# A decoder megakernel on one core: where the last encoder layer applies its third norm, and how top-k attention removes the scores that were not chosen

## The reference, cut to what matters

```python
xb = _layernorm(xb + o, g1[l], be1[l])            # first norm
ff = relu(xb @ W1[l].T + b1[l]) @ W2[l].T + b2[l]
xb = _layernorm(xb + ff, g2[l], be2[l])           # second norm
...
x = _layernorm(x + _L1_attn_ref(x, ...))          # third norm, once, behind the last layer
```

```python
scores = einsum('bthd,bghd->bhtg', Q, K) / sqrt(32)
scores = where(vision_mask, scores, -inf)
topv, topi = top_k(scores, 32)
probs = softmax(topv)
attn = zeros_like(scores).at[bi, hi, ti, topi].set(probs)
c_t = einsum('btg,bgd->btd', attn.mean(axis=1), x_vision @ Wv)
```

## Time and profile before

| what | value |
|---|---|
| time, median of 3 (lowest, highest) | 2394.77 us (2393.81, 2398.04) |
| the profiled execution | 2396.02 us, its span 2394.2 us |
| busy: PE, DVE, ACT, POOL | 88%, 63%, 30%, 34% of the span |
| encoder's last layer and its end | about 1508 to 1727 us |
| top-k attention, first `max` to the last `attend` | 1733.40 to 2050.49 us |

### The profile page before, as it was taken

How to read it: one execution, slowest core, us unless ns; L and a number is a source line. 1 busy time by engine, 2 the same in 40 slices (tenths; PEclk the granted TensorE clock), 3 DMA queues, 4 the chain that set the end, 5 groups by cost and what they waited for, 6 DMA issues and landing times.

```text
span 2394.2 us, 37754 instructions
## 1 busy us (share of the span) xinstructions
PE 2103.9 (88%) x15300; PEld 1469.6 (61%) x15300; DVE 1514.4 (63%) x3047; ACT 711.3 (30%) x1407; POOL 810.4 (34%) x726
## 2 busy tenths in 40 slices
PE   6988979999999978999999999988567767879986
PEld 2334337777766656888888888776445555446632
DVE  7998955566333325556556555666398998737556
ACT  6445324333311222232223222222142222121132
POOL 3242448966500014444444444432270000013101
PEclk9768689999899989999999999999766675889998
DMA  5222173222010027101001000100231110310001
GB/s 154 70 75 90 57 161 92 60 67 71 7 53 1 1 94 173 34 1 69 1 2 51 19 1 1 52 1 1 71 100 29 30 30 25 87 49 1 0 0 31
DMA packets 67181, 114.47 MB, mean 48 GB/s; under 512 B 34153, under 2 KB 58722, under 8 KB 65794
## 3 DMA queue, kind: packets, MB, share of 16 engines
q1 hardware_dynamic: 67010, 112.07, 16.3%
HBM read 91.56 MB, written 33.34 MB: 52 GB/s over the span
## 4 chain that ended last, share of the span: by engine, by line
PE 64%; DVE 25%; POOL 6%; issue 3%; ACT 2%; DMA 0%; SPq 0%; DVEq 0%; POOLq 0%; ACTq 0%
PE PS L1534 8%; PE PS L1550 8%; PE PS L1280 5%; PE PS L1258 4%; DVE top L2334 4%; DVE w_s L2343 4%; PE PS L2214 2%; DVE ln_st L270 2%; PE PS L2204 2%; PE PS L1447 2%; PE PS L1461 2%; PE PS L2143 2%; PE PS L892 2%; PE PS L879 2%; PE PS L409 2%
## 5 line engine op out<-in xcount | busy, mean ns | idle before, releaser
L289 POOL TENSOR_SCALAR ln_ve<-ln_mv 128x2 f32<-128x2 f32 (+1 forms) x87 | 20.0, 230 | 1195.5 <-DVE ln_mv L273 1195.4
L1807 POOL TENSOR_TENSOR q_x<-q_f,cols 128x2048 f32<-128x2048 f32 x56 | 217.9, 3911 | 9.7 <-ACT q_f L1638 8.0
L1762 DVE TENSOR_TENSOR p_x<-PS,cols 128x1024 f32<-128x1024 f32 x112 | 129.3, 1218 | 134.3 <-PE PS L1496 134.3
L1089 DVE TENSOR_REDUCE XD<-PS 112x2 f32<-112x750 f32 x128 | 120.0, 940 | 96.0 <-PE PS L879 95.6
L457 PE MATMUL PS<-bc_parts,ident 96*128 96x448 bf16 x256 | 106.0, 518 | 41.2 <-DVE st_h L691 28.0
L1048 ACT ACTIVATE e_t<-PS 125x672 f32<-125x672 f32 x128 | 93.5, 730 | 154.8 <-PE PS L892 154.8
L1337 DVE SCALAR_TENSOR_TENSOR XA<-PS,gate_w,XA 112x256 f32<-112x256 f32 x128 | 56.0, 480 | 125.6 <-PE PS L1280 125.6
L2096 PE MATMUL PS<-dg,e_p 112*125 112x112 f32 x384 | 80.1, 400 | 61.7 <-ACT dg L2292 61.7
L1625 ACT ACTIVATE wb<-PS,cols 128x256 f32<-128x256 f32 x224 | 90.8, 472 | 142.8 <-PE PS L1534 142.8
L879 PE MATMUL PS<-enc_w,q_s 32*112 32x375 f32 x512 | 130.6, 535 | 1.7 <-DVE XD L1089 1.7
L892 PE MATMUL PS<-q_s,enc_w 32*125 32x112 f32 x1536 | 121.9, 289 | 2.6 <-ACT e_t L1048 2.6
(11 more groups left out here) (366 smaller groups left out, 4710.6 us busy)
## 6 DMA issues: line engine op xcount, KB each, us to landing
k_full_scratch<-k_scratch SPq DMA_DIRECT2D x112, 112.0 KB, 2.9
v_all_scratch<-v_st SPq DMA_DIRECT2D x16, 750.0 KB
v_t<-v_all_scratch SPq DMA_DIRECT2D x16, 750.0 KB
t_ring<-k_full_scratch SPq DMA_DIRECT2D x8, 784.0 KB, 12.4
enc_w<-in_enc_w SPq DMA_DIRECT2D x2, 3072.0 KB, 11.2
wc<-in_enc_w SPq DMA_DIRECT2D x2, 3072.0 KB, 12.2
k_all_scratch<-k_st SPq DMA_DIRECT2D x16, 375.0 KB
enc_w<-k_all_scratch SPq DMA_DIRECT2D x64, 93.8 KB, 3.5
```

Of the source, the lines that this page charges most:

```text
L1089: dve.tensor_reduce(nm_w[0:T, g % 4, 64 * half + 16:64 * half + 49:32], PS[0:T, 2 * half:2 * half + 2, 0:S2], AX.X, ALU.max, negate=True). ...
L1762: last = dve.tensor_tensor(p_x[:, m, :, :, :], ps[1][:, m * P:(m + 1) * P].rearrange("p (h i) -> p h i", i=16).unsqueeze(2) .to_broadcast( ...
L1807: last = pool.tensor_tensor(q_x[:, c, :, :].rearrange("p t (h i) -> p t h i", i=16), q_f[:, k % 2, c, :].rearrange("p (t i) -> p t i", i=1 ...
```

## The change

**In the encoder**, for steps 21 to 27 only: the third norm leaves `second_norm`. The addition of xg0 and the statistics (`last_stats`) run at the end of the DVE's iteration, behind `first_norm`; the application (`last_apply`) runs in the next iteration, behind the turned and spread probabilities (p_x). `turn_second` and the copy of its result move one iteration later; `feed_out` waits for one copy less; the last `turn_second` calls no longer stand between `first_norm` and `feed_in`. The POOL does the root of the third norm at the end of its iteration.

**In top-k attention**: the DVE's L2353, L2356 and L2357 go. The ACT now also takes the exponential of what is left in w_s (FILL gives 0 there), and of the 32 largest with their sum; the POOL subtracts the former from e_p, which leaves the chosen ones, and makes the weights with a power of -1. w_s and top8 get a slot for each of four heads (before, two), with new waits x_rest and x_cut for their reuse. The PE takes keys two batches ahead, and the scores in two halves, one ahead of `attend` and one behind `gather`; `values` comes after them. The row transposes and copies are split over two batches, the POOL's norm work is cut into pieces between its subtractions, and the mask product is in bf16.

```diff
@@ enc_pe @@
             def feed_out(i):
                 if i >= 1:
-                    pe.wait_ge(ez_copied, i)
+                    pe.wait_ge(ez_copied, i if i <= LAST_0 else i - 1)
...
             def turn_second(i):
                 pe.wait_ge(n2_done, i + 1)
                 if i >= 1:
                     pe.wait_ge(ez_copied, i)
+                if LAST_0 <= i < STEPS - 1:
+                    pe.wait_ge(eg_added, i + 2)
...
-                if 0 <= k - 3 < STEPS and k != STEPS + 1:
+                if 0 <= k - 3 < LAST_0:
+                    turn_second(k - 3)
+                if LAST_0 <= k - 4:
+                    turn_second(k - 4)
+                if k == STEPS + 2:
                     turn_second(k - 3)
...
-                if k == STEPS + 1:
-                    turn_second(k - 3)
@@ enc_dve @@
-                    link(dve.tensor_tensor(x, x, xg0[:, 2 * r:2 * r + 2, :], ALU.add))
-                    normed(x).then_inc(n2_done, 1)
+            def last_stats(i):
+                link(dve.tensor_tensor(x, x, xg0[:, 2 * r:2 * r + 2, :], ALU.add))
+                return norm_stats(dve, link, [x[:, g, :] for g in range(2)], P)
...
+                if LAST_0 <= k - 3 < STEPS:
+                    last_apply(k - 3, waiting)
                 if 0 <= k - 2 < STEPS and k != STEPS:
                     second_norm(k - 2)
                 if 0 <= k - 1 < STEPS:
                     first_norm(k - 1)
                 if k == STEPS:
                     second_norm(k - 2)
+                if LAST_0 <= k - 2:
+                    waiting = last_stats(k - 2)
+            last_apply(STEPS - 1, waiting)
@@ s4x_pe @@
-            for b in range(B):
-                if b + 1 < B:
-                    if b >= 1:
-                        topk_keys(pe, b + 1)
-                    scores(b + 1)
-                    attend(b)
-                    gather(b)
-                    if b % QB == QB - 1:
-                        values(b // QB)
+            for b in range(B - 1):
+                if b + 2 < B:
+                    topk_keys(pe, b + 2)
+                    scores(b + 2, (0, 1))
+                attend(b)
+                gather(b)
+                if b + 2 < B:
+                    scores(b + 2, (2, 3))
+                if b % QB == QB - 1:
+                    values(b // QB)
@@ s4x_act @@
+            def rest_and_sum(b, h):
+                act.wait_ge(x_sel, XH * b + h + 1)
+                bias = neg_m[:, h:h + 1]
+                act.activation(w_s[:, h, :], w_s[:, h, :], ACT.Exp, bias=bias)
+                tops = top8[:, h, :, :].rearrange("t r v -> t (r v)")
+                act.activation(tops, tops, ACT.Exp, bias=bias, accum_out=e_sum[:, b % 2, h:h + 1])\
+                    .then_inc(x_rest, 1)
...
+                    if h == 1:
...
+                            if b + 1 < B:
+                                copy_keys(b + 1)
+                            weights(b - 1)
+                        rest_and_sum(b, 0)
+                        rest_and_sum(b, 1)
+                    elif h == 3:
...
+                            copy_attention(b - 1)
+                        rest_and_sum(b, 2)
+                        rest_and_sum(b, 3)
+                        if b >= 1:
+                            copy_context(b - 1)
@@ s4x_dve @@
-                        last = link.mark(dve.scalar_tensor_tensor(e, w_s[:, a, :], FILL, e, ALU.is_equal, ALU.mult,
-                                                                  accum_out=e_sum[:, b % 2, h:h + 1]))
-                link(dve.reciprocal(e_rs[:, b % 2, :], e_sum[:, b % 2, :]))
@@ s4x_pool @@
+                    pool.wait_ge(x_rest, n + 1)
+                    e = e_p[:, XH * (b % 2) + h, :]
+                    pool.tensor_tensor(e, e, w_s[:, h, :], ALU.subtract).then_inc(x_cut, 1)
+                    if h == XH - 1:
+                        link(pool.tensor_tensor(e_rs[:, b % 2, :], e_sum[:, b % 2, :], minus[:, :], ALU.pow))
```

More of the change, by code:

```diff
@@ L662, in ssm_dve @@
             dve.wait_ge(const_loaded, 80)
-            for k in range(3):
+            for k in range(4):
                 last = dve.tensor_copy(ident16[32 * k:32 * k + 32, 0:32], ident[32 * k:32 * k + 32,
@@ L1617, in copy_residuals, with copy_last @@
                         .then_inc(xg0_copied, 1)
+            def copy_last(i):
+                r = i % ROUNDS
+                act.wait_ge(ez_ready, i + 1)
+                for c in range(KC):
+                    last = act.copy(
+                        XF[:, c, :].rearrange("p (b t) -> p t b", b=B)[:, 16 * r:16 * r + 16, :],
+                        ps[3][:, c * RT:(c + 1) * RT].rearrange("p (t b) -> p t b", b=B))
+                last.then_inc(ez_copied, 1)
             def relu(i, half):
@@ L1645, in enc_act @@
                     act.copy(s_t[:, :], ps[0]).then_inc(st_copied, 1)
-                if 0 <= k - 3 < STEPS:
-                    layer, r = divmod(k - 3, ROUNDS)
+                if 0 <= k - 3 < LAST_0:
+                    r = (k - 3) % ROUNDS
                     act.wait_ge(ez_ready, k - 2)
[L1649 to L1657, removed]
+                    act.copy(XD[:, :, r * RT:(r + 1) * RT], ps[3].rearrange("p (c n) -> p c n", c=KC))\
+                        .then_inc(ez_copied, 1)
+                if LAST_0 <= k - 4:
+                    copy_last(k - 4)
+                if k == STEPS + 2:
+                    copy_last(k - 3)
                 if k < STEPS:
@@ L2076, in turn_rows, with scores @@
                 last.then_inc(m_ready, 1)
-            def scores(b):
+            def scores(b, heads):
                 pe.wait_ge(m_used, max(m_count("k", b), m_count("q", b // QB)) + 1)
-                for h in range(XH):
+                for h in heads:
                     n = XH * b + h
@@ L2122, in s4x_pe @@
             pe.wait_ge(e_prep, 3)
-            scores(0)
+            scores(0, range(XH))
             queries(2)
@@ L2258, in copy_context, with copy_values, weights @@
                 act.copy(m1[0:CR[1], 1, b * T:(b + 1) * T], bank[0:CR[1], T:2 * T]).then_inc(m_used, 1)
[L2259 to L2263, removed]
+            def copy_values(q):
+                for c in range(KC):
+                    act.copy(c_t[:, c, q * QT:(q + 1) * QT], m_bank(act, "ct", 2 * q + c)[:, 0:QT])\
+                        .then_inc(m_used, 1)
+            def rest_and_sum(b, h):
[5 more added lines that the diff above has]
+                    .then_inc(x_rest, 1)
+            def weights(b):
+                act.wait_ge(x_rs, b + 1)
+                for h in range(XH):
+                    last = act.activation(dg[:, b % 2, h, :], ident[0:T, 0:T], ACT.Copy,
+                                          scale=e_rs[:, b % 2, h:h + 1])
+                last.then_inc(x_dg, 1)
             def copy_rows(j):
@@ L2328, in s4x_dve @@
                                 dve.wait_ge(x_s_ready, n + 1)
+                                if b >= 1:
+                                    dve.wait_ge(x_rest, n - 3)
                             elif turn == 1:
@@ L2332, in s4x_dve @@
                                 link.after(cut[a])
[L2333 to L2334 removed]
+                            s = ps[h][0:T, 0:S2] if turn == 0 else w_s[:, h, :]
+                            found[a] = link.mark(dve.max(top8[:, h, turn, :], s))
                         if turn == 0:
```

152 lines of the change are left out of this document (89 added, 63 removed).

## The result

| | before | after |
|---|---|---|
| median, us | 2395.33 (2393.81 to 2398.04, 4 runs) | 2376.79 (2375.02 to 2381.71, 4 runs) |
| profiled execution, us | 2396.0 | 2375.02 (span 2372.8) |
| mean granted clock | 0.894 | 0.881 |
| first `max` to the start of the last `attend`, us | 317.1 | 326.5 |
| the same to the end of the last `attend`, us | 320.1 | 329.5 |

The kernel after takes 0.9925 of the time before (0.9913 to 0.9937): 18.5 us less, where I had forecast 54 less and a range of 29 to 86. The sign was right, the size wrong. Windows of the kernel after, columns as in the earlier trace rows: two steps of the encoder (third layer, last layer), the whole of top-k attention, and one batch of it.

The account below looks back on a forecast made before the run. It took the PE, plus the third norm in the last layer, to bound the encoder and the DVE top-k attention; 2396.0 - 26.5 (encoder) - 27 (top-k) = 2342.5, median 1.3 below: 2341 us, range 2309 to 2366.

Parts of the forecast that it names:

- The encoder: Encoder, steps 22 to 27: moving the third norm off the chain saves 26.5 us (25.2 to 27.9), clock included.
- steps 22 to 25: Encoder: each of four last-layer iterations loses the third norm's 3.13 us, 12.5 us less in all.
- step 26: Encoder: its interval loses the third norm too, with no later step's queries in its iteration, 3.6 us less.
- step 27: Encoder: `feed_in` no longer waits for all of `second_norm(26)` and starts 9.1 us earlier.
- the clock's share: Encoder, `feed_in(26)`: less PE idle time might keep the clock up, 0 to 2.7 us less, taken as 1.3.
- Rival 3: Encoder: L1743 ends too late behind the POOL's q_x, the norm stays on the chain, 12.5 us lost, 2354 us; chance 0.08.
- The DVE's part of top-k: Top-k attention: without the removed instructions the DVE needs 15.9 us per batch; DVE-bound, the stage is 261 us.
- The circle: Top-k attention: loop of ctx_f load, keys, scores, `attend` and gather through SP, DMA and PE, 18.4 us a turn.
- I take values between: Top-k attention: PE durations put between both clocks' values: keys 2.4, `attend` 5.1, gather 2.4 us.
- my upper bound: Top-k attention: a turn of the load-to-gather loop with the PE at 1.2 GHz throughout, 20.2 us.
- `values` falls mostly into the wait for the transfer: Top-k attention: `values`, 3.8 to 7.2 us, mostly hidden while the PE waits for the ctx_f load.
- Rival 2: Top-k attention: the load-to-gather loop runs at 1.2 GHz, 20.2 us a turn, stage 315 us, time 2368 us; chance 0.13.

Follow-up runs that it names:

- e1: Kernel before with only the encoder's part of the change, top-k attention as before: 2373.1 us, ratio to before 0.9894.
- e6: Kernel after with eight constant-data matmuls put into the PE's wait for ctx_f of each batch from the third on: 2328.5 us, ratio to before 0.9712.
- e10: Kernel after, unchanged, timed once more on another chip: 2374.1 us, ratio to before 0.9915.
- e7: Kernel after with the mask in f32 again instead of bf16: 2363.3 us, ratio to before 0.9855.
- e3: Kernel after with the load of ctx_f issued earlier in SP's queue, a gather sooner, still two buffers: 2323.2 us, ratio to before 0.9679.
- e4: Kernel after with four constant-data matmuls put into the PE's wait for ctx_f of each batch from the third on: 2343.1 us, ratio to before 0.9746.
- e9: Kernel after with ctx_f loaded early and the mask in f32: 2325.1 us, ratio to before 0.9709.

## Why the prediction was wrong

**The encoder was right.** Kernel after, the first layer product of the feed-forward part in steps 26 and 27 and what releases the latter:

```profile
1639.55 8.86 PE L1536 MATMUL PS<-wc 128*128 128x256 f32 x32 [0.67 <-ACT wc L1682]
...
1666.29 1.09 PE L1431 MATMUL PS<-ident,XA 128*128 128x128 f32 x4 [5.95 <-DVE XA L1719]
...
1668.91 9.99 PE L1536 MATMUL PS<-wc 128*128 128x256 f32 x32 [0.68 <-ACT wc L1682]
```

For steps 21 and 27 it starts at 1508.3 and 1700.08 in before (the earlier trace rows for the latter), at 1503.60 and 1668.91 in after: 191.7 us against 165.3, so 26.4 less. Forecast were 25.2 without the clock: steps 22 to 25 gave 12.5 of 12.5 (27.45 each), step 26 some 3.9 of 3.6, step 27 10.0 of 9.1 (29.4 us long). Only the clock's share went the other way. `feed_in(26)` got 0.75 us shorter (8.86 against 9.61 in the earlier trace rows), where I took 1.3; but `feed_in(27)`, with the PE idle for 5.95 us shortly before it, got 1.3 longer (9.99 against 8.70). So some 25 are left at the start of top-k attention, and e1 measures 25.

**Rival 3 didn't happen.** Kernel after, where the DVE and the POOL meet, the answer to the earlier trace rows:

```profile
1560.22 7.81 POOL L1833 TENSOR_TENSOR q_x<-q_f,cols 128x2048 f32<-128x2048 f32 x2
1560.62 0.35 DVE L1763 RECIPROCAL s_s<-s_s 128x32 f32<-128x32 f32 x1
1561.01 3.46 DVE L1764 TENSOR_TENSOR s_m<-s_m,s_s 128x512 f32<-128x512 f32 x1
...
1565.41 0.60 PE L1498 MATMUL PS<-ident,s_m 128*128 128x128 f32 x4
```

The softmax's product ends at 1564.47, 0.94 us ahead of the PE that reads it: the cover of 0.9 us that I had worked out.

**The DVE's part of top-k was right.** A batch keeps it busy for 15.82 us (15.9 forecast), the POOL's subtraction takes 0.98 (1.0), the ACT 7.26 per batch (at most 9.2), and `match_replace` keeps its 0.53 to 0.54 beside a working POOL. L2353 with its 2.68 us is gone. The section "Who interferes with whom" of the page SBUF — State Buffer, in the Trainium skill, says that a DVE instruction with at most one SBUF input, outside the two-port modes, doesn't contend with GpSimd; the trace agrees. Kernel after, a `match_replace` that starts while a subtraction is still going:

```profile
2019.19 0.98 POOL L2517 TENSOR_TENSOR e_p<-e_p,w_s 112x375 f32<-112x375 f32 x1
...
2019.90 0.54 DVE L2406 MATCH_REPLACE8 w_s<-top,w_s 112x375 f32<-112x375 f32 x1
```

Behind the last `match_replace` it was 5.4 us to the last `attend` (5.7 forecast).

**The circle was right in its form and mis-sized in its terms.** I had seen that the load now stands between gather and keys, and that no DVE shortens this. The step that failed is the one after it: "I take values between". The duration of each PE operation was taken between its values at the two clocks, by the mean clock of the stage in before. Against the chain above:

| term | forecast | measured |
|---|---|---|
| issue and landing of ctx_f | 6.0 | 6.1 to 6.5 |
| keys | 2.4 | 3.15 |
| scores and masks of two heads | 1.4 | 1.9 |
| `attend` | 5.1 | 5.3 |
| gather | 2.4 | 2.9 |
| copies and hand-overs | 1.1 | 1.1 |
| turn | 18.4 | 20.4 to 20.9 |

The landing, the term that had never been on a chain, came out at what the earlier trace rows gave for it (5.1 to 5.2 us). The turn is that of my upper bound, 20.2, with scores and masks of 1.9 us where it had 1.7. From the first gather to the last that a load waits for, after has thirteen turns (I had counted fourteen, 2.5 us too much), 276.2 us in all, where 18.4 each would make 239.2. Of the 37 us more, 29 are thirteen turns of 20.6 on average. The second mis-sized step was that "`values` falls mostly into the wait for the transfer": at 1.2 GHz it takes 7.2 us against a wait of 4.7 and adds 2.7 in each of three turns, 8 together. The stage is 36.5 us longer than the 290 of the forecast. Rival 2, the circle at 1.2 GHz, is what happened, and I gave it 0.13. Its own 2368 lacked the `values` and the last 0.2 to 0.4 us of a turn.

**Why a mean was the wrong value.** The clock isn't a property of the stage that one can carry over; here it hung on what the PE does while the load is under way. In e6 the same circle with the same load ran at 0.91, with six of thirteen turns at 14.5 to 15.1 us; in after it ran at 0.54 with turns of 20.5, none of them shorter than 20.4 (in e10, the same kernel, one was 18.3). Nor does a mean clock say which operations had it: a turn of e7 took 20.1 us at 0.66, where one at 0.50 took 21.5, since the high clock fell where the transfer covers it. The circle has an idle stretch of 4.7 us of the PE in each turn, at the transfer, ahead of the keys, which spoke for the lower value in all that stands behind it. Why e7's clock rises in some turns and after's does not is not shown beyond that. The page TensorE: Matmul & The Clock Gate of the Trainium skill ("HAM oscillation — how this bites in real kernels") says that a PE which waits for a transfer in each turn starts each one throttled; the trace of after agrees, at 0.50 in the window of a whole turn. I had cited it and let the 0.66 of before, where no load was waited for, outweigh it.

**The early stages** gave 4.7 us of the profiled difference ahead of step 21, where nothing was changed. The first `max` of kernels with the same encoder lies at 1703.7 (after), 1699.4 (e3), 1701.2 (e4), 1708.7 (e6) and 1702.2 (e10): a scatter between executions and no effect of the change.

## What to carry to other kernels

When an edit moves a consumer of a transfer ahead, look at where that transfer stands in its queue: a second buffer is worth nothing if its load is issued behind the wait of another one, and here moving the load ahead of that wait gave 54 us where the edit itself had cost 6. Work out a loop through a load at either clock and compare each with the rest of the batch. Don't fill in a stage's mean clock: ask which operations stand right behind the idle stretch of the PE, and put those at the lower level first. That is drawn from this one loop. Where such a loop sits at the lower clock, a PE operation made cheaper can cost time, so measure cheaper operations again after the wait is gone.

## What the runs showed of the hardware

- The same circle of a load and PE work ran at two levels: 14.67 us a turn at 2.4 GHz (e6) and 20.5 at 1.2 GHz (after). Matmuls on constant data in the place of the wait brought most of its turns to under 17 us, for 48 us in 2377.
- Masks in f32 instead of bf16 cost 1.0 us in a turn at the low clock and gained 13.5 us in all (e7), with a clock of 0.66 against 0.54; with the load early they gained nothing (e9).
- With the f32 masks of e7, a turn took 21.5 us at a granted clock of 0.50, 20.1 at a mean of 0.66 and 14.8 at 1.00: the mean doesn't give the turn by proportion, since it matters which operations run at the high clock.
- At 1.2 GHz throughout, the turns without `values` repeat within 0.5 us (20.4 to 20.9), and four runs of after spread over 6.7 us. Kernels whose clock moves from turn to turn can spread further: e4 over 22 us and e7 over 17 in four runs each.
